# Self-attention: the copy of the turned keys stands right behind the reciprocal on VectorE, and the loop over tiles is written out

## The reference, cut to what matters

```python
x = x + attn(layernorm(x))
# attn:
q, k, v = split(x @ W_qkv)
q = q * cos + rotate_half(q) * sin
k = k * cos + rotate_half(k) * sin
mask = (j <= i) & (j >= i - 128)
scores = where(mask, q @ k.T / sqrt(32), -max)
out = softmax(scores) @ v
return out @ W_out + b_out
```

## Time and profile before

| | us |
|---|---|
| median of 3 runs | 1675.92 |
| lowest and highest of them | 1671.69, 1676.97 |
| profiled execution, span | 1678.1 |
| PE busy | 1419.7 (85%) |
| DVE, ACT, POOL busy | 1050.1, 972.8, 759.6 |
| first scores of tile 0 to first scores of tile 15 (self-attention's main part) | 43.5 to 482.2 |
| end of self-attention's work | about 514 |
| all behind it (cross-attention, experts) | 1164 |

### The profile page before, as it was taken

How to read it: one execution, slowest core, us unless ns; L and a number is a source line. 1 busy time by engine, 2 the same in 40 slices (tenths; PEclk the granted TensorE clock), 3 DMA queues, 4 the chain that set the end, 5 groups by cost and what they waited for, 6 DMA issues and landing times. The chain is left out here.

```text
span 1678.1 us, 28691 instructions
## 1 busy us (share of the span) xinstructions
PE 1419.7 (85%) x9603; PEld 1053.1 (63%) x9603; DVE 1050.1 (63%) x2044; ACT 972.8 (58%) x1969; POOL 759.6 (45%) x492
## 2 busy tenths in 40 slices
PE   2889889899986767898898887856999999999990
PEld 2677777677764533444444433336999999999980
DVE  4666666667663533434443449855888888888880
ACT  3555455455552335674574575625777777777770
POOL 2344344444431013633533430003777777777762
PEclk9989999999997989998998998877999999999995
DMA  8000000000002276475466266055999999999986
GB/s 323 1 14 26 14 14 26 14 25 15 20 8 88 70 135 115 88 121 143 75 110 158 51 115 115 4 166 174 288 298 297 299 297 294 294 296 293 296 170 125
DMA packets 133106, 229.79 MB, mean 137 GB/s; under 512 B 17865, under 2 KB 51145, under 8 KB 132496
## 3 DMA queue, kind: packets, MB, share of 16 engines
q1 hardware_dynamic: 103184, 154.98, 34.0%
q0 software_dynamic: 29248, 72.53, 19.5%
q10 hardware_dynamic: 576, 0.98, 0.2%
HBM read 163.78 MB, written 71.83 MB: 140 GB/s over the span
## 5 line engine op out<-in xcount | busy, mean ns | idle before, releaser
L1045 ACT ACTIVATE shared<-xa_ring 128x1024 f32<-128x1024 f32 x256 | 247.0, 1030 | 94.1 <-PE xa_ring L1445 93.9
L1007 POOL TENSOR_TENSOR shared<-shared,xa_half 128x32 f32<-128x32 f32 x24 | 130.3, 5429 | 248.0 <-DVE shared L1168 248.0
L302 POOL TENSOR_TENSOR sa_prob<-sa_prob,sa_rinv 128x1024 f32<-128x1024 f32 x64 | 121.3, 1896 | 244.7 <-DVE sa_rinv L465 244.7
L1612 POOL DMA_INDIRECT ex_xg<-xn,token x128 | 173.9, 1359 | 82.2 <-issue 57.6
L360 ACT ACTIVATE sa_prob<-sa_sc_ps,sa_nmax 128x256 f32<-128x256 f32 x256 | 118.0, 473 | 111.1 <-DVE sa_nmax L452 111.1
L95 PE MATMUL ex_ba<-ex_xh,ex_wh 128*128 128x256 f32 x512 | 149.6, 292 | 4.4 <-DVE ex_xl L1726 3.7
L97 PE MATMUL ex_ba<-ex_xh,ex_wl 128*128 128x256 f32 x512 | 145.7, 285 | 0.0
L96 PE MATMUL ex_ba<-ex_xl,ex_wh 128*128 128x256 f32 x512 | 145.6, 284 | 0.0
L1457 PE MATMUL xa_out<-shared 128*17 128x512 f32 x1024 | 140.3, 621 | 0.5 <-ACT shared L1045 0.4
L1713 DVE TENSOR_TENSOR ex_wl<-shared,ex_wh 128x1024 fp32r<-128x1024 f32 (+1 forms) x128 | 116.9, 955 | 36.1 <-ACT ex_wh L1656 36.1
L452 DVE TENSOR_REDUCE sa_nmax<-sa_sc_ps 128x2 f32<-128x512 f32 x128 | 83.1, 687 | 66.5 <-PE sa_sc_ps L597 66.5
(11 more groups left out here) (223 smaller groups left out, 3939.7 us busy)
## 6 DMA issues: line engine op xcount, KB each, us to landing
shared<-in_L_ffn_gate_proj_dram SPq DMA_DIRECT2D x64, 384.0 KB, 5.7
shared<-in_L_ffn_up_proj_dram SPq DMA_DIRECT2D x64, 384.0 KB, 7.3
turned<-stage SPq DMA_DIRECT2D x64, 256.0 KB, 2.8
shared<-in_L_ffn_down_proj_dram SPq DMA_DIRECT2D x64, 256.0 KB, 5.0
xa_kT<-turned SPq DMA_DIRECT2D x96, 128.0 KB, 8.3
xa_qT<-turned SPq DMA_DIRECT2D x96, 128.0 KB, 10.5
shared<-in_L_ffn_down_proj_dram SPq DMA_DIRECT2D x64, 128.0 KB, 6.3
sa_x<-in_x_dram SPq DMA_DIRECT2D x16, 256.0 KB, 2.8
```

The lines of the kernel that those rows point to most:

```text
L302: pool.tensor_tensor(prob[:, 4 * g:4 * g + 4, :], prob[:, 4 * g:4 * g + 4, :], rinv[:, 4 * g:4 * g + 4].unsqueeze(2).to_broadcast([P, 4, 2 ...
L1007: pool.tensor_tensor(power[:, i], ms[:, i], half[:], ALU.pow).then_inc(s_pw, 1)
L1045: act.activation(prob[:, w % 2, 2 * i:2 * i + 2, :], ring[i][:], ACT.Exp, scale=D2 ** -0.5).then_inc(s_ex[i], 1)
L1612: pool.indirect_dma_start(out=xg[:, e % RING, j, :], out_offset=None, in_=xn3, in_offset=bass.IndirectOffsetOnAxis(token[:, at:at + 1], 0))\
```

## The change

In DVE's `tile`, the two branches with `take_k` move up: they now stand right behind the reciprocal in every group, ahead of `moments` (g = 1), of `low_qk` and `normalise` (g = 2) and of `low_x` (g = 3). `tiles` becomes a loop of Python over all 16 tiles, so every engine gets the code of each tile written out, without a hardware loop; `Tile` and the waits lose the cases in which a tile's number is a register. SP's loop over the sequences is written out too, and its loads and stores have fixed addresses. Nothing else changes: the same semaphores are counted to the same values.

```diff
         def tiles(engine, tile):
 
-            tile(Tile(0, 0))
-            with engine.Fori(0, B - 1) as b:
-                for i in range(1, T + 1):
-                    tile(Tile(b, i))
-            for i in range(1, T):
-                tile(Tile(B - 1, i))
+            for n in range(NT):
+                tile(Tile(0, n))
...
-                sp.dma_start(xs[:, t], x[bass.ds(b * T + t, 1), :, :].rearrange("a p d -> (a p) d")).then_inc(ld_x[t], 16)
+                sp.dma_start(xs[:, t], x[b * T + t]).then_inc(ld_x[t], 16)
...
-            with sp.Fori(0, B - 1) as b:
+            for b in range(B - 1):
...
                     dve.reciprocal(rinv[:, 4 * g:4 * g + 4], rsum[:, 4 * g:4 * g + 4]).then_inc(s_ri, 1)
+                    if g < 3:
+                        take_k(at, g + 1)
+                    elif nxt.exists():
+                        take_k(nxt, 0)
                     if g == 2 and nxt.exists():
                         low_qk(nxt, 0)
...
                     if g == 3 and at.ahead(2).exists():
                         low_x(at.ahead(2))
-                    if g < 3:
-                        take_k(at, g + 1)
-                    elif nxt.exists():
-                        take_k(nxt, 0)
                     if g == 3 and last.exists():
                         residual(last)
```

More of the change, by code:

```diff
@@ L226, in __init__ @@
             def __init__(self, b, t):
-                self.b, self.t = (b + t // T if t // T else b), t % T
+                self.b, self.t = b + t // T, t % T
                 self.n = self.b * T + self.t
@@ L236, in exists @@
             def exists(self):
-                return not isinstance(self.n, int) or 0 <= self.n < NT
+                return 0 <= self.n < NT
         def tiles(engine, tile):
-            tile(Tile(0, 0))
-            with engine.Fori(0, B - 1) as b:
-                for i in range(1, T + 1):
-                    tile(Tile(b, i))
-            for i in range(1, T):
-                tile(Tile(B - 1, i))
+            for n in range(NT):
+                tile(Tile(0, n))
         block = m.main_block()
@@ L257, in load @@
             def load(b, t):
-                sp.dma_start(xs[:, t], x[bass.ds(b * T + t, 1), :, :].rearrange("a p d -> (a p) d")).then_inc(ld_x[t], 16)
+                sp.dma_start(xs[:, t], x[b * T + t]).then_inc(ld_x[t], 16)
             def store(b, t):
                 sp.wait_ge(s_x1b, START + b * T + t + 1)
-                sp.dma_start(x1[bass.ds(b * T + t, 1), :, :].rearrange("a p d -> (a p) d"), xs[:, t]).then_inc(st_x[t], 16)
+                sp.dma_start(x1[b * T + t], xs[:, t]).then_inc(st_x[t], 16)
             sp.dma_start(odd_sum.rearrange("(n p) d -> p n d", p=P),
                          zero[:].unsqueeze(1).to_broadcast([P, NT, D])).then_inc(st_zero, 16)
-            with sp.Fori(0, B - 1) as b:
+            for b in range(B - 1):
                 for t in range(T):
@@ L288, in rotate @@
                 pool.wait_ge(s_t, START + 4 * n + 2 * i + 2)
-                if not isinstance(n, int) or n > 0:
+                if n > 0:
                     pool.wait_ge(s_lo, START + 2 * n + i - 1)
@@ L533, in project_out @@
                     k_read = 4 * (n + 3)
-                    if isinstance(n, int) and n + 2 >= NT:
+                    if n + 2 >= NT:
                         k_read = 4 * NT
@@ L548, in turn_heads @@
                         pe.wait_ge(s_lo, START + 2 * n + i + 1)
-                    if not isinstance(k, int) or k > 0:
+                    if k > 0:
                         pe.wait_ge((s_qe, s_ke)[i], START + k)
-                        if not isinstance(k, int) or k > 1:
+                        if k > 1:
                             pe.wait_ge(s_pe[i], START + k - 1)
@@ L560, in turn_prob @@
                 pe.wait_ge(s_pn, START + k + 1)
-                heads_read = k + 2
-                if isinstance(k, int):
-                    heads_read = min(heads_read, 4 * NT)
+                heads_read = min(k + 2, 4 * NT)
                 for i in range(2):
```

## The result

The changed kernel takes 1628.94 us (median of 4 runs, 1626.25 to 1631.54) where the kernel before takes 1673.81 beside it (1669.59 to 1676.97): a ratio of 0.9729 [0.9704, 0.9753], 2.7% faster. Predicted were 1627.0, between 1617 and 1641. The profiled execution went from 1678.1 to 1629.7.

The account below looks back on a forecast made before the run. PE was taken to bound the stage; 49.5 us in tiles 1 to 13 (waits 24.7, ends of turns 6.8, clock falls 18.0) plus 1 in tile 0, 50.5 off 1678.1, gave 1627 us, range 1617 to 1641.

Parts of the forecast that it names:

- The keys in group 2: `take_k` right behind the reciprocal costs VectorE nothing and ends PE's 2.48 us wait ahead of group 3: 1.92 us a tile.
- The new wait: At `turn_heads` of group 3, PE would wait 0.6 us for ACT, which comes last by a little.
- The period taken over from tile 14: Tiles 1 to 13 would each take 25.86 us, as tile 14 already does, in place of 27.76 without a clock fall.
- Groups 1 and 3: Moving `moments`, `low_x` and `residual` behind the copy costs nothing; perhaps 0.1 us a tile lost at group 3's end.
- The clock: PE's clock would no longer fall to half in tiles 1 to 13: ten falls, 1.8 us each, 18.0 in all.
- rival 1: In tiles 1 to 13 the clock falls as before, so all 18.0 us stay: 1645.6 us; chance 0.10.
- the 18.0 us of falls: Share of the gain in tiles 1 to 13 put down to ten falls of PE's clock, 1.8 us each.
- The loop written out: Without the branch, PE's 3.38 us idle at each of two ends of turns goes, 6.8 us; register instructions cost nothing.
- rival 3: Scores find another late input and tiles keep their waits; only ends of turns go, 10.4 us: 1667.7; chance 0.03.
- The sum: Tiles 1 to 13 win 49.5 us (24.7 waits, 6.8 ends of turns, 18.0 clock falls), tile 0 wins 1: 50.5.
- 2: Copy not free on VectorE: `low_qk` and `normalise` end later, 0.93 us won a tile, not 1.92: 1640.5; chance 0.10.
- 4: Slower: code run once is fetched anew, each of 15 steps between tiles stops PE 5.2 us: 1705; chance 0.03.

Follow-up runs that it names:

- Experiment 3: Changed kernel with the key copy of group 2 one place later, behind `low_qk` and ahead of `normalise`: 1629.0 us, ratio 0.9712 to the kernel before.
- experiment 2: Kernel before with loop written out, copy at its old place, nine extra mask matmuls in PE's group 3 wait for keys: 1653.24 us, ratio 0.9851.

## Why the prediction was right, step by step

**The keys in group 2: right, to 0.05 us.** The copy in time that VectorE stood still, `low_qk` 0.54 behind POOL's product, ACT last: each is in the rows of tile 6. The forecast for `turn_heads` was 248.18 on the old times, which is 223.81 on the new; it came at 223.84. The new wait was 0.45 us, where 0.6 was said, since PE itself came 0.2 later. The period taken over from tile 14, 25.86, is what came. Experiment 3 shows that the order counts: behind `low_qk` the copy costs 0.35 us a tile.

**Groups 1 and 3: right.** The tiles have no idle time there; `low_x` and `residual` lie beside PE's work.

**The clock: right that it holds, too sure of its price.** It is 1.00 in tiles 1 to 13, and experiment 2 shows that it is PE's idle time which brings the falls, so rival 1 is out for the right reason. But the 18.0 us of falls were those of one execution. The kernel before, profiled again, has 7 falls in this stretch in place of 10: 379.57 less 13 tiles of 27.77 and the 7.1 us of the two ends leaves 11.5 us, 1.6 each. The 49.5 us won in tiles 1 to 13 were 48.7 by the first pair of profiles (385.7 less 337.0) and 43.1 by the second (379.57 less 336.5).

**The loop written out: the wrong step.** 6.8 us for two ends of turns were put down to the hardware loop, as if a branch cost that, and rival 3's time rests on the same. They are real in the kernel before and gone in the changed one, but the copy alone removes them; the sum came out because the change does both. The time is indeed the branch's, 3.47 and 3.51 us there, but the same branch takes 0.22 and 0.24 once the copy has moved. The step failed where it took an idle time at a place for a fixed price of the instruction that stands there; the rows for the arriving code were not read. The register instructions, costed at nothing, cost 0.15 us in a tile that waits for the keys, because there they lay between the end of the wait and the scores; the 2.24 and 2.25 that I compared lie elsewhere.

**The sum.** 50.5 us predicted; 48.4 between the first two profiles (1678.1 and 1629.7), 50.3 between the second two (1674.8 and 1624.5), 44.9 and 49.6 by the medians. In the first pair: tiles 1 to 13 48.7; tile 0 0.95, where 1 was taken; a start 0.5 us later; tile 15 with self-attention's end 1.35 longer, at a clock of 0.87 in place of 0.94; the rest 0.6 shorter. In the second pair the rest is 4.4 shorter (1159.9 and 1155.5), in code that the change doesn't touch, so that its total comes so near to 50.5 is luck: tiles 1 to 13 gave 43.1 of the 49.5 forecast. One thing in tile 0 was not seen: PE waits there 2.55 us for ACT's copy ahead of `turn_heads` of group 3, the clock falls, and tile 1 takes 26.56 us for it.

```profile
67.86 1.39 PE L550 MATMUL sa_tn_ps<-ident,sa_stack 128*96 128x128 f32 x8 [2.55 <-ACT sa_pT L337]
```

**The rivals.** 2: did not come about, since `low_qk` kept its place behind POOL's product, ahead of the rotation. The two did slow each other, as before: the rotation took 1.73 us and `normalise` 1.50. 3: the keys were the late input. 4: straight code is fetched in 28 blocks from 43 to 520 us with no idle PE in front of the first scores of tiles 1 to 15; stops of 3.4 us and more stood only at taken branches of the loop, and not at all of those.

## What to carry to other kernels

When an engine feeds the bound, put first what the bound waits for, and look for instructions that only stand and wait for another engine: a copy in front of one of those was free here. Before you price a loop by the idle time at its end, read the branch's own time and whether code arrives there, and test the loop and the order apart: here one part held the whole gain. And price clock falls by several executions, since their number varies from one to the next where the waits do not.

## What the runs showed of the hardware that was not expected

- A hardware loop of PE can run from code at hand (no block in two turns of 103 us each, 0.22 to 0.24 us for a branch back) or fetch 8 or 9 blocks of 16 KB in each turn and stand idle 3.4 to 3.6 us at its end, in a branch of 3.5 to 3.8 us. The same instructions of PE do either: a change on VectorE alone switched it.
- Behind idle times of the same 2.3 to 2.5 us the clock fell to 1.2 GHz in 8, 5 and 3 of 13 cases in three profiles; behind 0.45 us it never did, nor behind the 0.94 us of experiment 3, nor with the waits filled by matmuls.
- VectorE and POOL slowed each other by more than the one wait seen beforehand: `low_qk`, `normalise` and the rotation together took 4.91 us side by side and 2.49 apart (1.72 + 1.48 + 1.71, and 0.68 + 0.54 + 1.27). The Trainium skill's rule in "SBUF — State Buffer" (Who interferes with whom), that the two engines share a port which one holds for a whole instruction, agrees with the direction; which of the three instructions holds it when, no row shows.
